# A gated feed-forward layer rebuilt from block products: seven instead of eight for each pair of batches

## What is computed

```python
x = x + _L0_ffn_ref(_layernorm(x), L0_ffn_w_gate_up, L0_ffn_w_down)

def _L0_ffn_ref(h_shard, w_gate_up, w_down):     # INTER = 2048, hidden 512
    gate_up = jnp.einsum('bsh,oh->bso', h_shard, w_gate_up)
    gate, up = jnp.split(gate_up, 2, axis=-1)
    h = jax.nn.silu(gate) * up
    return jnp.einsum('bsi,hi->bsh', h, w_down)
```

## Time and profile before

| | us |
|---|---|
| median of 3 runs | 3207.58 (3205.62 to 10657.96) |
| the profiled execution, its own time | 3208.35 |
| its span, first to last instruction | 3207.1 |
| mean granted TensorE clock | 0.978 of full |
| first feed-forward, norm of batch 0 to its last matmul | 1570.7 to 2112.4 |
| second feed-forward, the same | 2660.0 to 3202.1 |

### The profile page before, as it was taken

One profiled execution on the slowest core, in us unless ns is written; L12 is line 12 of the kernel. 1 busy time (PEld: TensorE's weight loads), 2 busy tenths in 40 slices (PEclk: granted clock), 3 DMA queues, 4 the chain that ended last, 5 costly groups with the idle time before them and its releaser, 6 DMA issues.

```text
span 3207.1 us, 44240 instructions
## 1 busy us (share of the span) xinstructions
PE 3056.9 (95%) x17041; PEld 1739.5 (54%) x17041; DVE 2126.6 (66%) x4092; ACT 1530.9 (48%) x2483; POOL 584.5 (18%) x429
## 2 busy tenths in 40 slices
PE   6999999999999799999799999989899888999999
PEld 3434334334333344444488888854344336888887
DVE  6998998998989777776444334446676766444343
ACT  4988888888888366666511111014343342111110
POOL 1000000000000445442100001004454451001000
PEclk9999999999999799999899999999999988999999
DMA  2000000000000000000110000043232312001001
GB/s 74 2 1 11 1 1 11 1 1 11 1 1 2 1 2 1 2 1 2 59 40 20 20 20 1 1 131 86 66 99 79 86 34 79 20 20 40 1 1 53
DMA packets 32855, 86.96 MB, mean 27 GB/s; under 512 B 7235, under 2 KB 7236, under 8 KB 30469
## 3 DMA queue, kind: packets, MB, share of 16 engines
q1 hardware_dynamic: 30022, 83.43, 8.8%
q10 hardware_dynamic: 2624, 0.69, 0.1%
HBM read 59.60 MB, written 20.97 MB: 25 GB/s over the span
## 4 chain that ended last, share of the span: by engine, by line
PE 43%; DVE 3%; DMA 2%; POOL 2%; issue 1%; ACT 1%; SPq 0%; ACTq 0%; POOLq 0%; DVEq 0%
PE ps L1201 22%; PE ps L1215 11%; PE ps L1578 3%; POOL ex_sum L1546 2%; PE ps L1642 1%; PE ps L1608 1%; PE ps L1566 1%; PE ps L1619 1%; PE ps L1593 1%; DMA k_stack<-halves 1%; DMA halves<-lo_b 1%; DVE out_t L1706 1%; DVE ffn_z L1227 1%; PE ps L1186 1%; DVE sums_sb L1705 0%
## 5 line engine op out<-in xcount | busy, mean ns | idle before, releaser
L655 DVE TENSOR_SCALAR pair_in<-key_words,row_words 128x512 f32<-128x512 f32 x1792 | 726.1, 480 | 44.2 <-PE ps L542 40.2
L740 ACT ACTIVATE pair_mid<-ps,row_bias 128x512 f32<-128x512 f32 x896 | 588.2, 688 | 133.2 <-PE ps L542 115.8
L542 PE MATMUL ps<-pair_in,w_hi 128*64 128x512 f16 x3584 | 584.3, 390 | 8.6 <-DVE pair_in L655 8.2
L1278 ACT ACTIVATE ffn_silu<-ps 128x512 f32<-128x512 f32 x128 | 76.2, 595 | 831.4 <-PE ps L1201 831.4
L1240 DVE TENSOR_TENSOR ffn_inner<-ffn_silu,ps 128x512 f32<-128x512 f32 x128 | 87.9, 687 | 550.5 <-PE ps L1201 550.5
L542 PEld LDWEIGHTS ps<-pair_in,w_hi 128*64 128x64 f16 x3584 | 202.2, 108 | 301.6 <-issue 66.8
L1003 DVE TENSOR_REDUCE maxes<-ps 128x2 f32<-128x1024 f32 x256 | 303.1, 1221 | 93.6 <-PE ps L919 92.5
L542 PE MATMUL ps<-pair_in,w_lo 128*64 128x512 f16 x1792 | 352.1, 388 | 0.0
L1047 ACT ACTIVATE ex<-ps 128x512 f32<-128x512 f32 x448 | 243.2, 595 | 118.9 <-PE ps L938 118.4
L1201 PE MATMUL ps<-ffn_z_hi,ffn_w_hi 128*128 128x512 f32 x1024 | 277.4, 393 | 1.7 <-ACT ffn_w_hi L1267 1.7
L1201 PE MATMUL ps<-ffn_z_hi,ffn_w_lo 128*128 128x512 f32 x1024 | 274.7, 390 | 1.9 <-POOL ffn_w_lo L1285 1.9
(11 more groups left out here) (209 smaller groups left out, 4420.0 us busy)
## 6 DMA issues: line engine op xcount, KB each, us to landing
ffn_raw<-in_w_ffn SPq DMA_DIRECT2D x14, 1536.0 KB, 6.7
q_stack<-halves SPq DMA_DIRECT2D x48, 256.0 KB, 5.1
k_stack<-halves SPq DMA_DIRECT2D x48, 256.0 KB, 5.9
halves<-hi_b SPq DMA_DIRECT2D x16, 512.0 KB, 2.6
halves<-lo_b SPq DMA_DIRECT2D x16, 512.0 KB, 3.6
out<-x SPq DMA_DIRECT2D x4, 1024.0 KB, 4.3
x<-in_x SPq DMA_DIRECT2D x6, 512.0 KB, 5.9
ffn_raw<-in_w_ffn SPq DMA_DIRECT2D x6, 512.0 KB, 4.7
```

Source lines behind the costliest of these rows:

```text
L542: s = nc.tensor.matmul(ps[F2 * half:F2 * half + F2, bank + which, :], w_part[:, :], words.rearrange("p (s two) -> p s two", two=2)[:, :, o ...
L655: s = nc.vector.tensor_scalar(p.pair_in[:, (4 * n + i) % N_PAIR, :], p.key_words[:, b % 2, :], p.row_words[:, b % 2, row:row + 1], None, A ...
L740: nc.scalar.activation(p.pair_mid[:, n % NG, which, :], ps[:, bank + which, :], ACT.Relu, bias=bias).then_inc(p.mid_made, 1)
```

## The change

Take two batches as one problem. The gate and up weights of one block of 128 inner columns, each cut in two along the hidden 512, are a 2x2 matrix of blocks; the normed inputs of the two batches, cut in the same way, are another. Their product is gate and up for both batches. Before, it takes 8 block products. Now it takes 7, by Winograd's form of Strassen's scheme: four sums of weight blocks (`sums`, on POOL, 256 columns each) and four differences of input blocks (`difference`, on DVE, 1024 columns each) are made first, and each block product is 6 matmuls (2 hidden blocks times 3). Some results are sums over several products. Products that go into the same result accumulate in the same PSUM bank; the others are added by DVE: `second_sum`, `fifth_sum`, `up_high`, `gate_sum`, `up_low`.

- The layer is now 32 units `s` (`UNITS_F`): 16 inner blocks for batches 0 and 1, then 16 for batches 2 and 3. The first unit of each pair is plain: 48 matmuls without sums. The other 30 have 42. The down matmuls (768) and the transposes are as before; a chunk's 48 down matmuls stand in even units, 24 behind product 2 (`side[0]`) and 24 ahead of product 4 (`side[1]`).
- The weights are loaded and split for each unit, so twice for a layer, gate/up and down weights in separate transfers (512 KB in pieces of 512 bytes, and 256 KB).
- The turned inputs lie in SBUF in full precision first (`z_t`); seven operands (`b_hi`, `b_lo`, 1024 columns each) are made of them, for each pair. High parts come from ACT, low parts from DVE, but of operands 3 and 7 from POOL.
- Product 1 is copied out by ACT (`first_copy`) before product 2 is added to its bank. Product 7 waits for `second_sum`, 3 for `fifth_sum`, 4 for `up_high`.
- gate_low is the gate of the pair's first batch, gate_high that of its second, and likewise for up and inner. The product of silu and up has both its inputs in SBUF now (`inner_high`, `inner_low`), and its high part is a copy on ACT, no longer a cast on DVE.
- Semaphores of the two layers are shared (`Since` adds what the first layer counted).

```diff
+PAIRS = B // 2
+UNITS_F = PAIRS * NI
+A_PLACE = {1: 0, 2: 1, 4: 2, 5: 3, 6: 4, 7: 5, 3: 6}
+PRODUCTS = (1, 6, 5, 2, 7, 3, 4)
+OPERANDS = (1, 2, 3, 8, 6, 5, 7, 4)
...
+    def behind(s):
+        steps = [("split_down", s)] + [("load_down", s + 2)] * (s + 2 < UNITS_F)
+        return steps + [("sums", s + 2)] * (s + 2 < UNITS_F and not plain(s + 2))
+    order = [("load_up", 0), ("load_down", 0), ("load_up", 1), ("load_down", 1)] + split(0) + load_up(2)
+    order += [("norm", 0)] + [("turned", 0, f) for f in range(ND)] + [("norm", 1), ("sums", 1)]
+    order += [("operand", 0, 1), ("operand", 0, 2)] + [("turned", 1, f) for f in range(ND)]
+    order += [("product", 0, 11), ("product", 0, 21), ("operand", 0, 3), ("operand", 0, 8), ("product", 0, 12),
+              ("product", 0, 22), ("difference", 0, 1), ("difference", 0, 2), ("operand", 0, 6), ("operand", 0, 5)]
+    order += split(1) + load_up(3) + [("gate_low", 0), ("difference", 0, 3), ("operand", 0, 7), ("difference", 0, 4),
+                                      ("operand", 0, 4), ("gate_high", 0), ("inner_low", 0), ("inner_high", 0),
+                                      ("low_low", 0), ("low_high", 0)] + behind(0) + [("norm", 2)]
+    for s in range(1, UNITS_F):
+        side = [[], []]
+        if s == 1:
+            side = [[("turned", 2, f) for f in range(ND)] + [("norm", 3)], [("turned", 3, f) for f in range(ND)]]
+        elif s % 2 == 0:
+            side = [[("down", s // 2 - 1, b, t) for t in range(NT)] for b in (0, 1)]
+        if plain(s):
+            order += [("product", s, 11), ("operand", 1, 6), ("operand", 1, 5), ("gate_low", s)] + split(s + 1)
+            order += load_up(s + 3) + [("product", s, 21)] + side[0]
+            order += [("product", s, 12), ("gate_high", s), ("difference", 1, 3), ("operand", 1, 7),
+                      ("difference", 1, 4)] + behind(s)
+            order += side[1] + [("inner_low", s), ("low_low", s), ("product", s, 22), ("operand", 1, 4),
+                                ("inner_high", s), ("low_high", s)]
+            continue
+        if s == NI - 2:
+            order += [("difference", 1, 1), ("difference", 1, 2)]
+        after = {n: [("operand", 1, 8 if n == 4 else n)] if s == NI - 1 else [] for n in (1, 2, 3, 4)}
+        order += [("product", s, 1), ("first_copy", s)] + after[1] + split(s + 1)[:1]
+        order += [("product", s, 6), ("second_sum", s)] + split(s + 1)[1:] + load_up(s + 3)
+        order += [("product", s, 5), ("fifth_sum", s), ("product", s, 2), ("gate_low", s)] + after[2] + side[0]
+        order += [("product", s, 7), ("up_high", s), ("product", s, 3), ("gate_sum", s), ("gate_high", s)] + after[3]
+        order += behind(s) + side[1] + [("inner_high", s), ("low_high", s), ("product", s, 4), ("up_low", s),
+                                        ("inner_low", s), ("low_low", s)] + after[4]
+    return order + [("down", UNITS_F // 2 - 1, b, t) for b in (1, 0) for t in range(NT)]
...
+        t_1, t_2, t_3, t_4 = z[:, 0:2, :], z[:, 2:4, :], z_t[:, 1, 0:2, :], z[:, 0:2, :]
+        b_11, b_21, b_12, b_22 = z_t[:, 0, 0:2, :], z_t[:, 0, 2:4, :], z_t[:, 1, 0:2, :], z_t[:, 1, 2:4, :]
+        operand_of = {1: b_11, 2: b_21, 3: b_22, 4: t_4, 5: t_1, 6: t_2, 7: t_3, 8: b_12}
...
+            elif kind == "product":
+                s, n = at
...
+                elif n == 2:
+                    pe.wait_ge(first_made, sevens_to(s))
+                elif n == 7:
+                    pe.wait_ge(second_made, sevens_to(s))
+                elif n == 3:
+                    pe.wait_ge(fifth_made, sevens_to(s))
+                elif n == 4:
+                    pe.wait_ge(up_high_made, sevens_to(s))
...
+                for which, (part, a_at, operand) in enumerate(factors):
+                    for m, (b_part, a_part) in enumerate(((b_hi, a_hi), (b_lo, a_hi), (b_hi, a_lo))):
+                        if m == 0:
+                            pe.wait_ge(w_hi_made, parts_to(s, part))
+                            pe.wait_ge(operand_hi, hi_of(s // NI, operand))
+                        elif m == 1:
+                            wait_for_low(pe, s // NI, operand)
+                        else:
+                            pe.wait_ge(w_lo_made, parts_to(s, part))
+                        for h in range(2):
+                            i = nc.tensor.matmul(bank, a_part[:, s % 2, a_at, h, :], b_part[:, place(operand), h, :],
+                                                 start=opens and (which, m, h) == (0, 0, 0),
+                                                 stop=(which, m, h) == (len(factors) - 1, 2, 1),
+                                                 skip_group_check=not opens)
+                i.then_inc(product_done, 1)
...
+            elif kind == "second_sum":
+                s, = at
+                dve.wait_ge(product_done, products_to(s, 6))
+                dve.wait_ge(first_made, sevens_to(s))
+                dve.wait_ge(gate_sum_made, sevens_to(s) - 1)
+                nc.vector.tensor_tensor(second[:, :], first[:, s % 2, :], bank_y(s), ALU.add).then_inc(second_made, 1)
...
+            elif kind == "up_high":
+                s, = at
...
+                nc.vector.tensor_tensor(up_1[:, :], fifth[:, :], bank_y(s), ALU.add).then_inc(up_high_made, 1)
+            elif kind == "gate_sum":
+                s, = at
...
+                nc.vector.tensor_tensor(gate_1[:, :], second[:, :], bank_z(s), ALU.add).then_inc(gate_sum_made, 1)
+            elif kind == "inner_high":
+                s, = at
+                dve.wait_ge(gate_high_made, s + 1)
...
+                nc.vector.tensor_tensor(gate_1[:, :], gate_1[:, :], up, ALU.mult).then_inc(inner_high_made, 1)
+            elif kind == "up_low":
...
+                nc.vector.tensor_tensor(up_0[:, :], first[:, s % 2, :], bank_y(s), ALU.add).then_inc(up_low_made, 1)
+            elif kind == "inner_low":
+                s, = at
+                dve.wait_ge(gate_low_made, s + 1)
...
+                nc.vector.tensor_tensor(up_0[:, :], gate_0[:, :], up, ALU.mult).then_inc(inner_low_made, 1)
+            elif kind in ("low_high", "low_low"):
+                s, = at
+                b, inner = (1, gate_1) if kind == "low_high" else (0, up_0)
+                dve.wait_ge(in_hi_made, 2 * s + (1 if bool(b) != plain(s) else 2))
+                nc.vector.tensor_tensor(in_lo[:, b, s % 2, :], inner[:, :],
+                                        in_hi[:, b, s % 2, :].bitcast(F32),
+                                        ALU.subtract).then_inc(in_made, 1)
...
+            elif kind == "first_copy":
+                s, = at
+                act.wait_ge(product_done, products_to(s, 1))
+                act.wait_ge(inner_low_made, s - 1)
+                nc.scalar.activation(first[:, s % 2, :], bank_x(s), ACT.Copy).then_inc(first_made, 1)
...
+            elif kind == "gate_high":
+                s, = at
...
+                else:
+                    act.wait_ge(gate_sum_made, sevens_to(s))
+                nc.scalar.activation(gate_1[:, :], bank_z(s) if plain(s) else gate_1[:, :],
+                                     ACT.Silu).then_inc(gate_high_made, 1)
+            elif kind in ("inner_high", "inner_low"):
...
+                act.wait_ge(inner_high_made if b else inner_low_made, s + 1)
+                act.wait_ge(down_done, 2 * NT * (s // 2))
+                nc.scalar.activation(in_hi[:, b, s % 2, :], inner[:, :], ACT.Copy).then_inc(in_hi_made, 1)
...
+            if kind == "sums":
+                s, = at
+                i = s % 2
+                gate, up = raw_up[:, i, :, 0, :], raw_up[:, i, :, 1, :]
+                pool.wait_ge(up_loaded[i], 16 * (s // 2 + 1))
...
+                nc.gpsimd.tensor_tensor(sums[:, 0], up[:, 0:2], up[:, 2:4], ALU.add).then_inc(sums_made, 1)
+                nc.gpsimd.tensor_tensor(sums[:, 2], gate[:, 0:2], up[:, 0:2], ALU.subtract).then_inc(sums_made, 1)
+                pool.wait_ge(sums_made, made + 2)
+                nc.gpsimd.tensor_tensor(sums[:, 1], sums[:, 0], gate[:, 0:2], ALU.subtract).then_inc(sums_made, 1)
+                pool.wait_ge(sums_made, made + 3)
+                nc.gpsimd.tensor_tensor(sums[:, 3], gate[:, 2:4], sums[:, 1], ALU.subtract).then_inc(sums_made, 1)
+                pool.wait_ge(sums_made, made + 4)
...
+            elif kind == "split_down":
+                s, = at
+                pool.wait_ge(down_hi_made, s + 1)
+                nc.gpsimd.tensor_tensor(d_lo[:, s // 2 % 2, s % 2, :], raw_down[:, s % 2, :],
+                                        d_hi[:, s // 2 % 2, s % 2, :].bitcast(F32),
+                                        ALU.subtract).then_inc(down_lo_made, 1)
```

More of the change, by code:

```diff
@@ L1162, in feed_forward @@
[L1162 to L1170 removed]
+        if part not in k.ffn_flags:
+            k.ffn_flags[part] = k.flag(f"ffn_{part}")
@@ new lines, in feed_forward, with products_before, products_to, sevens_to @@
+        differences_before = {4: 4, 5: 1, 6: 2, 7: 3}
```

(22 more changed lines are left out.)

390 lines of the change are left out of this document (265 added, 125 removed).

## The result

| | us |
|---|---|
| before, median of 4 | 3208.01 (3205.62 to 10657.96) |
| after, median of 4 | 3264.96 (3257.17 to 3267.84) |
| ratio | 1.0176 (95%: 1.0153 to 1.0200) |
| predicted | 3224, range 3155 to 3275 |
| profiled execution after, its span | 3263.07, 3261.5 |

What follows compares the result with a forecast made beforehand. PE's number of matmuls was taken as the bound; a layer sums to -40.8 + 27 + 12 + 4 + 6 = +8, both layers +16, giving 3224 us from 3208.35, range 3155 to 3275.

Steps and rivals of the forecast that it cites:

- the middle: Units 15 and 16, new operands for batches 2 and 3: gaps costing 4 us a layer, ends 1 and 8.
- the opening: From the norm to unit 1's end: 50.4 us, 12 us a layer more than before, ends 6 and 20.
- The chain at a unit's end: Odd-to-even unit borders: product 2 waits for first_copy, 1.9 us at 14 borders, 27 us a layer, ends 10 and 38.
- The saving: Gate and up products: 180 fewer matmuls a layer at 0.2267 us each, saving 40.8 us a layer.
- The rival that the chain hides: Unit ends: first_copy comes in time through overlap; -22 us a layer, 3164 us; chance 0.22.
- each meeting with POOL costs 2.07 us: Rival at odd units: two DVE waits for POOL each, 58 us a layer instead of 15, 3310 us; chance 0.04.
- DVE beside POOL: DVE operations with two SBUF inputs wait for POOL's running instruction; gap grows from 0.95 to some 2.0 us.
- then first_copy waits behind all of unit 0's tail: Opening walk, unit 1: after its low weights at 29 us, first_copy is held on ACT to 36.7 us.
- Unit 16 has 21.8 us of PE work for the rest: Middle: beyond unit 15's gaps of 1.6 and 1.1 us, unit 16's PE work was to cover the remaining operands.
- The tail: Last down matmuls wait for unit 31's inner parts, 5.4 us behind product 4: 6 us a layer, ends 4 and 9.
- The loads: Weight loads, 768 KB for each 15 us unit, issued a unit ahead: costed at nothing, some 20 us of cover.
- The clock rival: Unit borders: each of 28 gaps followed by a stretch at 1.2 GHz, 76 us, 3300 us; chance 0.08.

Runs made afterwards that it cites:

- experiment 5: Changed kernel with first_copy ahead of inner_low at odd-to-even borders, second batch's down matmuls first without waiting for low_low, product 22 in bank 6: 3214.49 us, ratio 1.0014.
- experiment 2: Changed kernel with one added wait: in odd units POOL's split_down waits until inner_low is made; 3236.62 us, ratio 1.0086 to before.
- experiment 3: Changed kernel with product 22 of the two plain units in PSUM bank 6 instead of the next unit's bank; 3256.24 us, ratio 1.0147 to before.
- Experiment 7: Against experiment 6: unit 1's weight split ahead of unit 0's last two products, first two differences moved from unit 14 to units 10 and 12; 3187.81 us, ratio 0.9931.
- experiment 6: Against experiment 5: batches 2 and 3 normed and turned in units 4 to 7, unit 1's product 1 and first_copy ahead of unit 0's tail; 3202.37 us, ratio 0.9976.

## Why the prediction was right and wrong

The step that failed is **the middle**, the term of the sum that I sized at 4 us a layer, with an upper end of 8. It measured 15.2 us in the first layer and 11.4 in the second, because I walked through two waits in unit 15 and there were six, in units 14 to 17. That is 19 of the 38 us missed. Another 10 are attention B, which I had put at nothing, and 6 the opening. The chain at a unit's end, on which most of the working went, came out as forecast. By parts:

| us a layer | predicted | layer 1 | layer 2 |
|---|---|---|---|
| fewer matmuls | -40.8 | -40.8 | -40.8 |
| chain at a unit's end | 27 | 26 | 28 |
| opening | 12 | 16.6 | 13.1 |
| middle | 4 | 15.2 | 11.4 |
| tail | 6 | 7.4 | 7.3 |
| sum | +8 | +24.4 | +19.0 |
| the stage, measured | | +24.7 | +18.8 |

That the sums meet the stages within 0.3 us is closer than two profiles of one kernel agree.

- **The saving** (-40.8 a layer) was right. 16681 matmuls against 17041 are 360 fewer, and experiment 5 has a pair of units at 30.46 us where the count gives 29.92.
- **The chain at a unit's end** (27 us a layer) was right in place and size: in even units behind first_copy, 1.9 us each predicted and 2.0 measured, 13 times instead of 14 and so 26 us in the first layer. POOL's share is 0.78 of each wait by experiment 2, where my walk had 1.1 to 1.3 ahead of the overlap. The rival that the chain hides is excluded; so is that each meeting with POOL costs 2.07 us.
- **DVE beside POOL.** In layer 1 the four operations with both inputs in SBUF take 0.74 (inner_high, at a moment when POOL is mostly idle), 0.90, 0.87 and 0.93 us in the mean, and those with one input in PSUM 0.677 to 0.687:

```profile
L1492 DVE TENSOR_TENSOR ffn_in_lo<-ffn_up,ffn_in_hi 128x512 fp32r<-128x512 f32 x32 | 29.7, 927 | 21.7 <-ACT ffn_in_hi L1563 21.6
...
L1487 DVE TENSOR_TENSOR ffn_up<-ffn_gate,ffn_up 128x512 f32<-128x512 f32 x30 | 27.0, 898 | 3.1
...
L1454 DVE TENSOR_TENSOR ffn_up<-ffn_fifth,ps 128x512 f32<-128x512 f32 x30 | 20.6, 687 | 33.3 <-PE ps L1374 33.3
```

  The rule that I drew on, the Trainium skill's "SBUF — State Buffer", Who interferes with whom, is borne out by this: an operation that meets a POOL instruction ends some 0.55 us after that instruction (1691.02 after 1690.47, 1692.87 after 1692.32), whatever its own start; over both layers all 83 operations of L1487 and L1492 that have both inputs in SBUF, start beside a POOL instruction and take over 0.8 us end 0.55 us after it.
- **The opening** (12 us) measured 16.6: unit 1 ends at 1626.26, 54.9 us behind the norm (predicted 50.4), less 32.6 for the old opening and 5.7 for the added matmuls and transposes. The walk was right as far as unit 1's low weights (28.8 us behind the norm, predicted 29) and for the end of first_copy (36.7, predicted 36.7); product 11 started at 12.5, predicted 14.3, and unit 0 ended at 24.0, predicted 25.4 (the 14.3 and 48 matmuls are 25.2). What failed in this walk is "then first_copy waits behind all of unit 0's tail": I let products 6 and 5 run ahead of it unhindered. Product 6 waits for `inner_high` of the plain unit, whose product 22 stands in its bank, and then 12 matmuls run at 0.43 instead of 0.23 us, so product 2 starts at 40.4 and not at 36.7. Taking the wait away alone helps nobody (experiment 3), since first_copy stands right behind it. In the second layer the same two waits are there (3.2 and 5.5 us), and the old opening was longer, 33.9 us for 32.6: it comes to 13.1.
- **The middle** (4 us, ends 1 and 8) measured 15.2, nearly twice its upper end. From product 2 of unit 14 to that of unit 18 there are 78.4 us (1821.94 to 1900.31). 270 matmuls (two pairs and the 6 that plain unit 16 has more) are 61.2 us, and the regular wait in unit 18 is 2.0: 15.2 are left, of which the six waits above are 10.7, and the 8 matmuls at the lower clock behind the last of them 1.6; the rest is half a us for each wait, as the steady pair has it too (2.0 us between starts for a wait of 1.44). The two that I named, in unit 15, were 1.15 and 0.46 us (predicted 1.6 and 1.1). I looked at nothing in unit 14, where two differences of 1024 columns take 1.21 and, beside POOL, 3.21 us (I had 1.2 for such an operation) and hold DVE's sums and with them the down additions, and in unit 17, where the bank of product 22 is waited for again. Experiment 7 moves these two differences away, and the wait in unit 14 (4.4 us in experiments 5 and 6) is gone; experiment 3 removes the wait for the bank. "Unit 16 has 21.8 us of PE work for the rest" was wrong: two waits of 1.6 and 2.1 us.
- **The tail** (6 us) measured 7.4: 5.4 us between the starts more than usual, as predicted, then 9 matmuls at the lower clock, 2 us.
- **The loads** cost nothing: 4.0 and 2.7 us to land, no product waits for one in the steady stretch.
- **The clock rival**: 26 gaps of 1.4 us left the clock whole (1.00 in the window). The lower level came in or behind gaps of 3.2 us in the opening, 2.7 in unit 17 and 5.3 in the tail. That rival is out for the steady stretch, and right at the irregular borders. One ground that I gave against it, slices at 9, was a poor reading: a slice is 80 us, and it shows 9 for the kernel before although 2174.8 to 2181.6 in it has a clock of 0.50.
- **Attention B** was not in the sum at all; I took a stage whose code stays as unchanged in time. It gave 10.3 us, about a quarter of the miss.
- **The sum.** Of the 38 us by which the span's difference (54.4) exceeds the predicted 16, 27 lie in the two feed-forwards, at opening, middle and tail, and 10 in attention B.

## What to carry to other kernels

When an algorithm saves work on the bounding engine and pays with a longer chain between engines, price each border of the schedule apart, the irregular ones above all: here the regular borders were foreseen to 0.1 us each, and the middle alone made half of the miss. For each matmul group ask for every earlier reader of its bank, in the irregular units too. Where two-input SBUF operations of DVE stand in the critical chain, keep POOL's instructions out of that moment: one wait on POOL gave back 20 us in the feed-forwards, and a reordered list turned the loss into a gain of 0.7%.
